# Value products of a cross-attention in blocks of three or four key tiles, in place of one or two

## The reference

```python
q = (x @ Wq + bq).reshape(b, t, NUM_HEADS, HEAD_DIM)
k = (inp @ Wk + bk).reshape(b, s, NUM_HEADS, HEAD_DIM)
v = (inp @ Wv + bv).reshape(b, s, NUM_HEADS, HEAD_DIM)
attn = jnp.einsum('bthd,bshd->bhts', q, k)
attn = jax.nn.softmax(attn / jnp.sqrt(jnp.float32(HEAD_DIM)), axis=-1)
out = jnp.einsum('bhts,bshd->bthd', attn, v).reshape(b, t, DIM)
```

## Time and profile before

| | us |
|---|---|
| median of 3 runs (4836.34 to 4844.47) | 4839.96 |
| profiled execution | 4841.48 |
| its span | 4839.6 |
| TensorE matmul busy | 3934.6 (81%) |
| VectorE busy | 3448.6 (71%) |
| ScalarE busy | 2863.0 (59%) |
| mean granted TensorE clock | 0.853 |

### The profile page before, as it was taken

How to read it: one execution, slowest core, us unless ns; L and a number is a source line. 1 busy time by engine, 2 the same in 40 slices (tenths; PEclk the granted TensorE clock), 3 DMA queues, 4 the chain that set the end, 5 groups by cost and what they waited for, 6 DMA issues and landing times. The chain is left out here.

```text
span 4839.6 us, 83868 instructions
## 1 busy us (share of the span) xinstructions
PE 3934.6 (81%) x34310; PEld 1295.2 (27%) x34310; DVE 3448.6 (71%) x3258; ACT 2863.0 (59%) x4073; POOL 258.7 (5%) x183
## 2 busy tenths in 40 slices
PE   6897478988898855888988898479747988898885
PEld 2563222222222212222222222135422222222221
DVE  4332488888888615888888885389848888888871
ACT  1332157777777741677777777335414777777774
POOL 3000000000000010000000000234310000000000
PEclk9556579999998985899999989789957999999998
DMA  2000310111111012110111010100041111011100
GB/s 83 1 0 11 70 22 13 24 24 24 16 21 24 4 37 59 23 24 13 23 24 24 13 24 4 43 19 5 3 81 16 19 24 24 14 23 24 24 2 20
DMA packets 103596, 114.10 MB, mean 24 GB/s; under 512 B 58672, under 2 KB 93712, under 8 KB 98256
## 3 DMA queue, kind: packets, MB, share of 16 engines
q1 hardware_dynamic: 103248, 109.19, 13.3%
HBM read 83.56 MB, written 25.60 MB: 23 GB/s over the span
## 5 line engine op out<-in xcount | busy, mean ns | idle before, releaser
L1510 DVE TENSOR_REDUCE chunk_max<-max_scores 128x2 f32<-128x1024 f32 (+1 forms) x2496 | 2801.6, 1179 | 534.5 <-PE max_scores L1399 408.3
L1497 ACT ACTIVATE probs<-scores 128x512 f32<-128x512 f32 (+1 forms) x3231 | 2471.6, 809 | 907.8 <-PE scores L1425 751.9
L1425 PE MATMUL scores<-queries,key_ring 49*128 49x512 bf16 x4800 | 1288.4, 404 | 244.0 <-ACT probs L1497 129.5
L1452 PE MATMUL values_sum<-probs,values 128*9 128x256 f32 x19584 | 1446.6, 402 | 1.7 <-ACT probs L1497 1.7
L1399 PE MATMUL max_scores<-key_ring,queries 48*128 48x512 bf16 (+1 forms) x4992 | 979.0, 411 | 216.1 <-DVE chunk_max L1510 154.2
L1452 PEld LDWEIGHTS values_sum<-probs,values 128*9 128x9 f32 x19584 | 386.8, 91 | 893.6 <-issue 626.1
L1425 PEld LDWEIGHTS scores<-queries,key_ring 49*128 49x128 bf16 x4800 | 313.1, 95 | 1141.7 <-ACT probs L1497 877.6
L1399 PEld LDWEIGHTS max_scores<-key_ring,queries 48*128 48x128 bf16 x4992 | 249.7, 97 | 645.7 <-DVE chunk_max L1510 555.9
L1057 ACT ACTIVATE probs<-scores 128x512 f32<-128x512 f32 x256 | 138.5, 592 | 106.1 <-PE scores L1009 106.1
L1524 DVE COPY values_sum_s<-values_sum 128x256 f32<-128x256 f32 x48 | 20.1, 418 | 235.0 <-PE values_sum L1452 235.0
L1083 DVE TENSOR_REDUCE chunk_max<-max_scores 128x1024 f32 (+1 forms) x128 | 154.9, 1213 | 23.6 <-PE max_scores L965 23.4
(11 more groups left out here) (176 smaller groups left out, 1944.1 us busy)
## 6 DMA issues: line engine op xcount, KB each, us to landing
key_ring<-k_parts SPq DMA_DIRECT2D x96, 300.2 KB
key_ring<-k_parts SPq DMA_DIRECT2D x96, 200.1 KB
k_parts<-k_part SPq DMA_DIRECT2D x108, 128.0 KB, 2.3
key_ring<-k_parts SPq DMA_DIRECT2D x96, 100.1 KB
o_whole<-values_sum_s SPq DMA_DIRECT2D x48, 128.0 KB, 8.0
queries<-q_parts SPq DMA_DIRECT2D x36, 128.0 KB
context<-in_ctx_t SPq DMA_DIRECT2D x1, 3202.0 KB, 17.5
q_parts<-q_part SPq DMA_DIRECT2D x12, 256.0 KB, 2.8
```

Source lines behind the costliest of these rows:

```text
L1425: return pe.matmul(sc[:, g % 3, :], keys(rows, h, P * t, P * (t + 1)), qb[rows, q], start=True, stop=True)
L1452: mm = pe.matmul(acc[32 * b:32 * b + WV, 0:QBLOCK], vb[rows, h, t, :], pr[rows, slot, QBLOCK * (b % 2):QBLOCK * (b % 2 + 1)], start=(t == ...
L1497: act.activation(pr[:, a % RING:a % RING + b - a, :], sc[:, a % 3:a % 3 + b - a, :], ACT.Exp)\
L1510: dve.tensor_reduce(mx[:, h % 2, c, :, j], mxb[:, u % 2, :, 0:w], AX.X, ALU.max)\
```

## The change

Value tiles are now handed out on every fourth step only (n = 3, 7, 11, ...), at most four at a time. As four steps make six slots, three tiles are the rule; behind a change of head, where tiles were held back, there are blocks of four. Nothing else is edited; which tiles are ready is decided as before, and the number of matmuls, exponentials and reductions stays the same.

```diff
--- before.py
+++ after.py
@@ -1300,12 +1300,12 @@
 
     done, total = [], 0
     for op in range(NOPS):
-        if op % 2 == 1 and op >= 3:
+        if op % 4 == 3:
             slots = slots_through(op - 2)
             ready = tiles_in(slots)
             if slots % HEAD_SLOTS < HOLD:
                 ready = min(ready, NTILE * (slots // HEAD_SLOTS))
-            total = max(total, min(ready, total + 2))
+            total = max(total, min(ready, total + 4))
         done.append(total)
     return done
```

## The result

The changed kernel takes 5086.02 us (median of 4 runs, 5060.29 to 5106.39), the kernel before 4838.15 (4 runs): a ratio of 1.0512, 95% interval 1.046 to 1.0563. That is slower by 248 us (223 to 272 by the interval), where 279 were forecast. The profiled execution took 5086.84 us at a mean granted clock of 0.858, before 0.853: a lower mean clock is not the reason.

The account below looks back on a forecast made before the run. VectorE was taken as the bound, by little. Groups with units (81.4 us), last heads (7.1) and four-tile blocks (4.3) made 93 us per layer, 279 in three: 5119 us, range 4940 to 5220.

Parts of the forecast that it names:

- The bound and the two loops: Undisturbed groups: VectorE binds before; after, VectorE's banks close two-then-one units at 3.89 us, ScalarE's ring one-then-two at 3.88.
- the 3.28: Groups without max units before the change, reckoned with the two-tile block: 3.28 us, checked against 3.29 in the trace.
- The last heads: About the last 1.2 heads per layer, without max units: groups 3.71 us against 3.29, 7.1 us per layer.
- The chain to the row maxima: Next head's row maxima travel by DMA; this wait shrinks as groups ahead lengthen, giving back 1.2 us per head.
- the four-tile blocks: Right behind changes of head, 20 per layer, half at full clock: 10 x 0.43 = 4.3 us per layer.
- the 4.01: Mean changed group with max units: 3.90 and 5.03 us weighed about 10 to 1, +0.39 us per group.
- the 3.62: Mean group before, in one head's undisturbed stretches: 3.62 us, from 1.173 us per unit; 13.9 such groups per head.
- the narrow groups: Groups at the four narrow units of a head's last key chunk: 3.2 to about 3.8 us, 0.8 per head.
- groups with two and two units: Fourth unit also waits for the second reduction, 1.14 us more: 5.03 us; 22 such groups per layer.
- The change of head: About 1.6 groups at the lower clock go from 6.0 to 6.3 us: 0.5 per head, before the chain's give-back.
- The Trainium skill's rule: Tiling-mode switches drain TensorE; if TensorE were the bound, fewer switches save 161 us: 4680 us, rival chance 0.07.
- Rival 4, the colder clock: TensorE's new gaps draw the clock down in a tenth more groups, 170 us on top: 5290 us, chance 0.07.

Follow-up runs that it names:

- runs 3 to 6: Kernel before and changed kernel, both with halved reductions (4626.65 and 4860.79 us), then both with halved exponentials (4785.15 and 5028.62 us).
- run 4: Changed kernel with VectorE reducing only the first half of each chunk of max scores: 4860.79 us, 1.0008 of the kernel before.
- run 11: Changed kernel with its value block behind step 4k in place of 4k + 3: 5209.98 us, 1.0618 of the kernel before.
- run 12: Kernel before with one-tile value blocks behind three of four steps, the third behind step 4k in place of 4k + 2: 4924.23 us, ratio 1.0152.
- run 7: Kernel before with blocks of up to four tiles allowed, still every two steps: 4866.72 us, ratio 1.0011.
- Runs 8 and 12: Kernel before with one-tile blocks behind three of four steps, the third behind step 4k + 2 (4917.39 us, 1.013) or 4k (4924.23 us, 1.0152).

## Why the prediction was right

*The bound and the two loops*: right, and each shown alone (runs 3 to 6). In the first cross-attention I took the starts of all value blocks. Of 247 groups with units in the changed kernel 143 last 3.9 us, 15 last 3.7 and 13 last 5.0; before, 114 of 241 last 3.5 or 3.6 and 37 last 3.8. Forecast were 3.89, 3.88 and 5.03.

*A simpler form*: three score banks let one pair of steps (S2 and S1) be in flight, so each pair costs at least 1.51 us, ScalarE's ring, and at least TensorE's own work in that pair. The changed kernel with one then two units has 0.67 us of work in the first pair and 2.37 in the second: 1.51 + 2.37 = 3.88. With two then one it would be 1.51 + 2.16, near the 3.73 of run 4, and VectorE's banks lift it to 3.89. Before, it is 1.95 at most and 1.51: 3.46, below VectorE's 3.52. But it is a floor and no more. Without units it gives 3.02 before and 3.45 after, and the groups take 3.29 and 3.73: the S1 scores wait for the short exponential, and the block stands behind them. In run 11 it gives 1.96 + 1.51 = 3.47, and the groups take 3.95. The prediction's way, one line from wait to wait, has the 3.28, the 3.71 and most of the 3.95 (4.0 to 4.2 expected). This form came after run 12; no run was made to test it.

*The last heads*: 3.71 forecast, 3.73 measured; 7.1 us per layer forecast, 7.1, 7.3 and 8.7 measured (from the copy of the 15th head to that of the 16th).

*The chain to the row maxima*: it gives back 21 us in its own line (41 if VectorE's "remote" waits, which lie near the change of head too, belong to it, which is not shown) against 54 forecast.

*The term that was mis-sized*: the mean head got longer by 5.3, 4.1 and 4.9 us in the three stages, where 5.5 and 0.3 for the four-tile blocks were summed. All heads but the last grew by 219 us together where 257 were summed: 38 us, more than the 31 by which I was high. Laid group against group, the 13 groups in the middle of a head last 3.67, 3.66 and 3.70 us before and 4.02, 4.01 and 4.00 after. So the 4.01 was right, and the base was too low: the 3.62 and the 3.2 of the narrow groups came from one head. Per head these 13 groups cost 4.3 us more, where the prediction's terms give 5.4 (11.7 x 0.39 and 0.8 for the narrow ones); over 45 heads that is some 46 us too much. One part of it: groups with two and two units were set at 5.03 against the mean of 3.62, but those away from a change of head already took 4.35 us before. The change of head cost 0.5 us net, about what was summed, though the chain gave back less than forecast there.

*The Trainium skill's rule that changing the tiling mode drains TensorE* (TensorEngine Tiling (Array Packing), Key Properties), cited against the forecast: the block of three does cost 1.42 and not 3 x 0.55, so a switch is saved as the rows of before had it. It lies in time in which TensorE waits: its idle before scores, released by exponentials, is 497.0 us in the page above, 129.5 before.

*Rival 4, the colder clock*: small but there. One of the signs of being wrong was that the granted clock falls between the changes of head, and it did. Where a group has two and two units, TensorE waits longest, and 10 of the 45 such groups away from a change of head fall to the lower level, where none did before:

```profile
1562.89 0.39 PE L1399 MATMUL max_scores<-key_ring,queries 48*128 48x512 bf16 x2 [0.74 <-DVE chunk_max L1510]
...
1563.43 2.40 PE L1452 MATMUL values_sum<-probs,values 128*9 128x256 f32 x24
...
1565.76 0.61 PE L1425 MATMUL scores<-queries,key_ring 49*128 49x512 bf16 x2
```

The same block takes 2.33 us in place of 1.42 and the group 5.93 in place of 5.03. With the groups behind them that are still at the lower level, 19 in all, I put the cost at some 19 us of the 245 in the trace, an estimate from their lengths against 5.03 and 3.89. All time at the lower level in the three stages is 478 us, before 471: less of it falls at the changes of head, so the mean clock does not show it.

## What to carry to other kernels

Work that nobody waits for is not free on an in-order engine: it delays all that stands behind it. Of the five places tried for the value tiles, the one of before, a block for every turn of the ring, was the best (run 7 is level with it); one long block per two turns was slower wherever it stood, and so were three short ones. With a ring that holds one turn, each turn costs at least the larger of the consumer's time and the producer's, and slack of one turn can't be lent to the next; summing the engine's work over several turns hides that. That is a floor: the time itself comes from following each loop from wait to wait, for every pattern of work that occurs, as the loop that closes can be another one in each. Before batching for fewer switches, compare what is saved per switch (here 0.2 us) with the slack that the emptied turn leaves unused (here 0.6 to 0.8 us).

## What the hardware showed that was not expected

Halving the columns of the value products made the kernel before 4.7% slower, with a mean granted clock of 0.67 and stretches at 0.50 of 283, 198, 191 and 181 us in which TensorE counts as 98 to 99% busy. Busy time alone does not tell whether the clock comes back: in the kernel before, with full products, it was back within 20.5 us each time. In the changed order, the same halved products kept a mean of 0.761. Why the clock stayed low is open.

Two unlike loops of nearly one length (3.89 and 3.88 us) can lie over each other: removing either one by itself moved the distance between the kernels only from 248 to 234 and 243 us. Runs 8 and 12 met such a pair again, at 3.68.
